# Expert gates of 13 batches computed as sums on VectorE, with list building moved and two layouts changed

## The reference

```python
x = x + tanh(g_xattn) * attention(ctx_1024, layernorm(x))   # 8 heads of 128; keys: context and latents, 512 in all
n = layernorm(x)
gates = (n @ Wg + bg) / (1 + 1e-6)                          # 256 features -> 8 experts
weights, indices = top_k(gates, 2); weights = softmax(weights)
h = silu(n @ W1[e] + b1[e]);  y = h @ W2[e] + b2[e]         # per expert e, 256 -> 1024 -> 256
x = x + tanh(g_ffn) * sum(weights * y[indices])
```

## Time and profile before

| what | value |
|---|---|
| median of 3 runs | 1513.13 us (1512.32 to 1515.56) |
| profiled execution, its own time | 1508.33 us |
| its span, first to last instruction | 1506.6 us |
| PE busy | 1483.4 us (98%) |
| DVE busy | 1165.3 us (77%) |
| ACT busy | 950.7 us (63%) |
| POOL busy | 581.0 us (39%) |
| granted TensorE clock, mean | 0.998 |

### The profile page before, as it was taken

The page is one execution under the profiler, slowest core; times in us unless marked ns, Lnnn a source line. Parts: engine busy times, 40 slices in busy tenths (PEclk is TensorE's granted clock), DMA queues, the critical chain, the costliest instruction groups (busy, mean ns, idle before and its releaser), DMA issues. The chain is left out here.

```text
span 1506.6 us, 29833 instructions
## 1 busy us (share of the span) xinstructions
PE 1483.4 (98%) x10326; PEld 1369.4 (91%) x10326; DVE 1165.3 (77%) x2753; ACT 950.7 (63%) x2058; POOL 581.0 (39%) x650
## 2 busy tenths in 40 slices
PE   9999999999999999999999999999999999999997
PEld 7888898898898998888888989888999999999996
DVE  7888787878878787887878788777767776666685
ACT  6565556556565565655555565656778777777775
POOL 4323433233342323333333343223455455544552
PEclk9999999999999999999999999999999999999999
DMA  6010202011010110101011010002657655555563
GB/s 198 29 36 22 38 20 50 22 36 43 22 50 8 50 43 23 36 22 50 8 50 43 22 36 22 8 23 91 156 133 202 175 128 131 133 148 140 127 184 78
DMA packets 70576, 106.92 MB, mean 71 GB/s; under 512 B 11513, under 2 KB 55606, under 8 KB 70302
## 3 DMA queue, kind: packets, MB, share of 16 engines
q1 hardware_dynamic: 54462, 85.98, 17.4%
q0 software_dynamic: 15824, 18.98, 8.0%
q10 hardware_dynamic: 144, 0.05, 0.0%
HBM read 86.64 MB, written 18.35 MB: 70 GB/s over the span
## 5 line engine op out<-in xcount | busy, mean ns | idle before, releaser
L942 POOL TENSOR_SCALAR probs<-probs,rsum 128x512 f32<-128x512 f32 x256 | 176.0, 700 | 622.4 <-DVE rsum L1641 622.0
L1162 ACT ACTIVATE pt_hi<-turn 128x512 fp32r<-128x512 f32 x256 | 139.1, 595 | 238.5 <-PE turn L1318 232.7
L968 POOL DMA_INDIRECT out_rows<-yo,token x71 | 127.1, 1790 | 182.5 <-DVE yo L1817 163.7
L1766 DVE TENSOR_TENSOR ht_lo<-hs,ht_hi 128x512 fp32r<-128x512 f32 x142 | 98.2, 691 | 112.2 <-ACT ht_hi L1129 111.1
L1635 DVE TENSOR_REDUCE smax<-score 128x1 f32<-128x512 f32 x256 | 168.3, 684 | 8.5 <-PE score L195 8.3
L1061 ACT ACTIVATE probs<-score,nbias 128x512 f32<-128x512 f32 x256 | 173.2, 686 | 1.7 <-DVE nbias L1637 1.7
L1893 DVE TENSOR_TENSOR pt_lo<-turn,pt_hi 128x512 fp32r<-128x512 f32 x256 | 164.3, 683 | 12.2 <-ACT pt_hi L1162 12.2
L1120 ACT ACTIVATE hs<-ph,vecs 128x256 f32<-128x256 f32 (+1 forms) x284 | 114.4, 458 | 88.7 <-PE ph L195 81.9
L193 PE MATMUL py<-w_hi,ht_lo 128*128 (+1 forms) x568 | 162.6, 286 | 2.2 <-DVE ht_lo L1766 2.2
L194 PE MATMUL py<-w_lo,ht_hi 128*128 (+1 forms) x568 | 160.6, 283 | 0.0
L195 PE MATMUL py<-w_hi,ht_hi 128*128 (+1 forms) x568 | 160.6, 283 | 0.0
(11 more groups left out here) (246 smaller groups left out, 4720.7 us busy)
## 6 DMA issues: line engine op xcount, KB each, us to landing
w_raw<-in_L_ffn_W SPq DMA_DIRECT2D x45, 1024.0 KB, 5.2
spread<-mean_and_factor SPq DMA_DIRECT2D x15, 512.0 KB, 3.6
xhat_rows<-rows SPq DMA_DIRECT2D x16, 264.0 KB, 2.2
x_raw<-in_x SPq DMA_DIRECT2D x16, 256.0 KB, 3.0
c_raw<-in_ctx SPq DMA_DIRECT2D x16, 256.0 KB, 3.2
out_rows<-x SPq DMA_DIRECT2D x16, 256.0 KB, 2.2
z_turned<-in_x_turned SPq DMA_DIRECT2D x15, 256.0 KB, 3.9
z_turned<-in_ctx_turned SPq DMA_DIRECT2D x15, 256.0 KB, 4.4
```

What stands on the lines that cost most here:

```text
L942: last = pool.tensor_scalar(probs[n % 2][:, t, :], probs[n % 2][:, t, :], rsum[:, n % 2, t:t + 1], 1.0, ALU.mult, ALU.mult)
L968: pool.indirect_dma_start(out=A["out"], out_offset=bass.IndirectOffsetOnAxis(ap=token[:, u:u + 1].bitcast(U32), axis=0), in_=yo_of(t)[:, s ...
L1162: act.activation(pt[0][:, 2 * t:2 * t + 2, :], turn[t][:, :].rearrange("p (j i) -> p j i", j=2), ACT.Copy).then_inc(s_pthi, 1)
L1766: dve.tensor_tensor(lo[:, :], hs[n % N_HS][:, :], hi[:, :].bitcast(F32), ALU.subtract).then_inc(s_hlo, 1)
```

## The change

1. For batches 0 to 12 the units "t" and "g" are gone from PE, and so is ACT's copy of "t". `dots` computes each gate on DVE: one `scalar_tensor_tensor` multiplies 256 features of a row by the weights of one expert and sums them into `gates`. 16 such instructions make a batch (8 experts, 2 tiles of rows): in step 3, three behind `kt_lo` and one ahead of `ot_lo`; in each of steps 4 and 5, one ahead of `kt_lo`, three behind it, one ahead of `ot_lo` and one behind it. `largest` adds the bias itself.
2. For these batches `largest`, `choose` and `weigh`, ACT's `exp_gap` and the unit "r" come one step later, `find_places` in step 0 of the next batch, and `list_tokens` after step 5 of the next batch.
3. The counts use fp32r operands (`chosen`, and rounded copies of two constant matrices, made once by ACT).
4. From the second transfer on, means and factors are laid in DRAM by kind and row, so that `centre` and `normalise_turned` read contiguous values. They were 32 bytes apart. The write is now two transfers of single values.
5. The gate weights are loaded once, spread over all partitions (1 MB), early in the kernel.

```diff
+DOT_B = EARLY_B - 1
...
-        if h == T_STEP and 1 <= b < B:
+        if h == T_STEP and DOT_B < b < B:
             units.append(("t", b - 1))
-        if h == G_STEP and 1 <= b < B:
+        if h == G_STEP and DOT_B < b < B:
             units.append(("g", b - 1))
-        if h == W_STEP and 1 <= b < B:
+        if h == (W_STEP if b > DOT_B else W_STEP + 1) and 1 <= b < B:
             units.append(("r", b - 1))
...
-            spread=nc.dram_tensor("mean_and_factor", (B, P, 2, JT), F32, kind="Internal").ap(),
+            spread=nc.dram_tensor("mean_and_factor", (B, 2 * KEYS), F32, kind="Internal").ap(),
...
-        chosen = late("chosen", [P, E, TT])
+        chosen = late("chosen", [P, E, TT], F32R)
...
+        below_r = late("below_r", [P, P], F32R)
+        ones_r = late("ones_r", [P, P], F32R)
...
+        wg_wide = sb("wg_wide", [P, E, D])
+        dot_junk = sb("dot_junk", [P, 4, D])
...
+                if c == 1:
+                    sp.dma_start(dram["spread"][c].rearrange("(i n) -> i n", n=2 * JT),
+                                 norms[:, :, :].rearrange("i r j -> i (r j)")).then_inc(s_norms_out, 16)
+                else:
+                    by_kind = dram["spread"][c].rearrange("(r j i) -> r i j", r=2, j=JT)
+                    with nc.allow_non_contiguous_dma(reason="a value of each row"):
+                        for r in range(2):
+                            sp.dma_start(by_kind[r], norms[:, r, :]).then_inc(s_norms_out, 16)
+                sp.wait_ge(s_norms_out, norms_out(c))
                 if c == 1:
                     weights_split(sp, "k1")
                 else:
                     sp.wait_ge(s_zin, KD * (c - 1))
-                sp.dma_start(spread[:, :, :, :].rearrange("p i r j -> p (i r j)"),
-                             dram["spread"][c].rearrange("i r j -> (i r j)").partition_broadcast(P)).then_inc(s_spread, 16)
...
+            weights_split(sp, "o1")
+            sp.dma_start(wg_wide[:, :, :].rearrange("p e d -> p (e d)"),
+                         A["gate_rows"].rearrange("e d -> (e d)").partition_broadcast(P)).then_inc(s_wg_wide, 16)
...
-                if h == L_STEP and 1 <= b < B:
+                if h == L_STEP and DOT_B < b < B:
                     list_tokens(b - 1)
+                if h == G_STEP + 1 and 2 <= b < DOT_B + 1 or i == H * (DOT_B + 1):
+                    list_tokens(b - 2)
...
+                    act.wait_ge(s_routing, N_ROUTING)
+                    act.activation(below_r[:, :], below[:, :], ACT.Copy).then_inc(s_round, 1)
+                    act.activation(ones_r[:, :], ones[:, :], ACT.Copy).then_inc(s_round, 1)
...
-                if i % H == E_STEP and 1 <= i // H < B:
+                if i % H == (E_STEP if i // H > DOT_B else E_STEP + 1) and 1 <= i // H < B:
                     exp_gap(i // H - 1)
...
-                    pe.wait_ge(s_routing, N_ROUTING)
+                    pe.wait_ge(s_round, 2)
                     pe.wait_ge(s_chosen, at + 1)
                     ch = chosen[:, :, :].rearrange("p e t -> p (e t)")
-                    pe.matmul(dst[:, 0:E * TT], below[:, :], ch, start=True, stop=True)
-                    last = pe.matmul(dst[:, E * TT:2 * E * TT], ones[:, :], ch, start=True, stop=True)
+                    pe.matmul(dst[:, 0:E * TT], below_r[:, :], ch, start=True, stop=True)
+                    last = pe.matmul(dst[:, E * TT:2 * E * TT], ones_r[:, :], ch, start=True, stop=True)
...
+            def dots(b, first, end):
+                dve.wait_ge(s_xn, b + 1)
+                dve.wait_ge(s_wg_wide, 16)
+                own.wait()
+                for q in range(first, end):
+                    e, t = divmod(q, TT)
+                    own.mark(dve.scalar_tensor_tensor(out=dot_junk[:, q % 4, :], in0=rows[b % 2][:, t, 0:D], scalar=1.0,
+                                                      in1=wg_wide[:, e, :], op0=ALU.mult, op1=ALU.mult,
+                                                      accum_out=gates[:, t, e:e + 1]))
             def largest(b):
-                dve.wait_ge(s_read, read_number["g", b] + 1)
+                if b < DOT_B:
+                    own.wait()
+                    own.mark(dve.tensor_tensor(gates[:, :, :], gates[:, :, :],
+                                               bg[:, :].unsqueeze(1).to_broadcast([P, TT, E]), ALU.add))
+                    own.wait()
+                else:
+                    dve.wait_ge(s_read, read_number["g", b] + 1)
...
-                own.mark(dve.tensor_tensor(by_rows, by_rows, spread[:, :, 0, :].rearrange("p i j -> p j i"), ALU.add))
+                own.mark(dve.tensor_tensor(by_rows, by_rows, spread_of(c, 0), ALU.add))
             def normalise_turned(c, k):
                 own.wait()
                 by_rows = zin[:, k, :].rearrange("p (j i) -> p j i", j=JT)
-                dve.tensor_tensor(by_rows, by_rows, spread[:, :, 1, :].rearrange("p i j -> p j i"), ALU.mult).then_inc(s_zin, 1)
+                dve.tensor_tensor(by_rows, by_rows, spread_of(c, 1), ALU.mult).then_inc(s_zin, 1)
             for i in range(STEPS + 2):
                 b, h = i // H, i % H
...
                 if i == STEPS:
                     lo_h(0)
                     find_places(B - 2)
+                summed = 1 <= b <= DOT_B
+                if summed and h == G_STEP:
+                    dots(b - 1, 4, 5)
+                if summed and h == G_STEP + 1:
+                    dots(b - 1, 10, 11)
                 for u in steps[i]:
                     if u[0] in "kq":
                         read_unit(*u)
...
                             normalise_turned(b + 1, 1)
                         if h == R_STEP + 1 and 1 <= b < B:
                             x2_moments(b - 1)
+                        if summed and h == T_STEP:
+                            dots(b - 1, 0, 3)
+                        if summed and h == G_STEP:
+                            dots(b - 1, 5, 8)
+                        if summed and h == G_STEP + 1:
+                            dots(b - 1, 11, 14)
                 if i < STEPS:
                     reciprocal_sum(i)
                 if i == STEPS - 1:
...
                 if i in (2, 3):
                     normalise_turned(1, i - 2)
                 for u in steps[i]:
+                    if u[0] == "o" and summed and h == T_STEP:
+                        dots(b - 1, 3, 4)
+                    if u[0] == "o" and summed and h == G_STEP:
+                        dots(b - 1, 8, 9)
+                    if u[0] == "o" and summed and h == G_STEP + 1:
+                        dots(b - 1, 14, 15)
                     if u[0] in "vogr":
                         read_unit(*u)
+                if summed and h == G_STEP:
+                    dots(b - 1, 9, 10)
+                if summed and h == G_STEP + 1:
+                    dots(b - 1, 15, 16)
                 if i == 0:
                     lo_weights(dve, "dve", "q1")
...
                 if 1 <= b < B:
                     for at, part in ((R_STEP, residual), (G_STEP, largest), (E_STEP, choose), (W_STEP, weigh),
                                      (L_STEP, find_places)):
-                        if h == at and i != STEPS - 1:
+                        if h == at + (summed and at >= G_STEP) and i != STEPS - 1:
                             part(b - 1)
+                if h == 0 and 2 <= b < DOT_B + 2:
+                    find_places(b - 2)
                 if i == HOME_STEP:
                     find_home()
                 if i == GATHER_STEP - 1:
...
+    arrays["in_gate_rows"] = np.ascontiguousarray(np.asarray(inputs["L0_ffn_Wg"]).T)
```

More of the change, by code:

```diff
@@ L442, in layer @@
                        o0=alloc(raws, "o0_raw", [P, H // 2, D]), o1=alloc(raws, "o1_raw", [P, H // 2, D]))
-        spread = sb("spread", [P, P, 2, JT])
+        spread = sb("spread", [P, 2 * KEYS])
+        wg_wide = sb("wg_wide", [P, E, D])
+        dot_junk = sb("dot_junk", [P, 4, D])
         x2, rows = [x2_0, x2_1], [rows0, rows1]
@@ L529, in layer @@
         s_padz, s_chosen, s_place, s_routing = sem("padding_zero"), sem("chosen"), sem("places"), sem("routing_consts")
+        s_round = sem("routing_consts_rounded")
+        s_wg_wide = sem("gate_weights_wide_in")
         s_dve, s_pool = sem("dve_self"), sem("pool_self")
@@ L644, in added, with norms_out, spread_of @@
             return min(t, WIDE) if half else t
+        def norms_out(c):
+            return 16 + 32 * (c - 1)
+        def spread_of(c, r):
+            if c == 1:
+                return spread[:, :].rearrange("p (i r j) -> p r j i", r=2, j=JT)[:, r]
+            return spread[:, :].rearrange("p (r j i) -> p r j i", r=2, j=JT)[:, r]
         def by_step(function, t):
@@ L739, in spread_norms @@
                 sp.wait_ge(s_z, c + 1)
-                sp.dma_start(dram["spread"][c], norms[:, :, :]).then_inc(s_norms_out, 16)
-                sp.wait_ge(s_norms_out, 16 * c)
+                if c == 1:
```

(9 more changed lines are left out.)

## The result

| | median | range | runs |
|---|---|---|---|
| before | 1513.37 us | 1512.32 to 1515.56 | 5 |
| after | 1505.12 us | 1500.99 to 1506.03 | 5 |

The ratio is 0.9935, 95% interval [0.9925, 0.9945]: faster by 0.65%, some 8 us. I had forecast 1517 and gave "faster" 0.38. The profiled execution took 1503.53 us, its span is 1501.8; against the profiled one of before that is -4.8.

The account below looks back on a forecast made before the run. PE was taken to bound the kernel: 20.8 us gained there against 13 batches of 1.9 us waiting gave +3.9 on 1508.3, 1512.2. With the median 4.8 above the profiled execution, the forecast was 1517, range 1490 to 1534.

Parts of the forecast that it names:

- What leaves PE: On PE, "t" and "g" save 1.31 us per batch, "r" 0.25; together 20.8 us, between 17.0 and 24.4.
- In place: one engine waits for the other: Steps 3 to 5: DVE's dots and POOL's work exclude each other on shared ports, making PE wait 1.9 us per batch.
- POOL's pair isn't opened: Rival: both halves of POOL's normalisation run before a waiting dot; 3.5 us per batch, 1538; chance 0.16.
- So a dot costs 0.45 to 0.56 and I take 0.45 to 0.50: DVE's time for each dot including the accumulator's read, 7.2 to 8.0 us per batch.
- The walk: One batch followed through steps 3 to 6 on DVE and POOL: 1.7 us of waits at 0.45 a dot, 2.4 at 0.50.
- the transposes' share: In step 5 PE's transposes wait for POOL's pair, delayed by dots: another 0.4 us per batch.
- The sum: PE's gain of 20.8 us against 13 batches of 1.9 us waiting: +3.9 us on the profiled execution.
- my likeliest case: Waits between 1.7 and 2.4 us per batch in steps 3 to 6: 1510 to 1527, chance 0.42.
- the hidden dots: Rival: POOL doesn't hold the dots, 1492; hidden in whole or good part, 1490 to 1508, chance 0.34.
- the point from which it decides: Waits below 1.6 us per batch, 20.8/13, decide for the rival that the dots are hidden.
- What is moved, all at nothing: List transfers, later routing work, new layout of means and factors, gate weights and ACT's copies: no cost.

Follow-up runs that it names:

- x1: Changed kernel with POOL's subtraction `kvt_lo` left out from batch 2 on, so later batches use an old low part; 1498.99 us, ratio 0.9889.
- x2: Changed kernel with the same 16 dots per batch moved within steps 3 to 5, none around `kt_lo` in step 4; 1502.9 us, ratio 0.991.
- x3: Kernel before with only the counts changed to fp32r operands; 1514.24 us, ratio 0.9989.
- x5: Changed kernel with the dots' scalar read from a column of ones in SBUF instead of the constant 1.0; 1511.34 us, ratio 0.9979.
- x4: Changed kernel with means and factors laid as before, 32 bytes apart and written in one transfer; 1509.66 us, ratio 0.9958.
- x12: x2 with the four list transfers in two pairs, behind POOL's pairs of the third and sixth steps; 1485.22 us, ratio 0.9824.
- x13: x2 with one list transfer each behind POOL's pairs of the third, fifth, sixth and seventh steps; 1484.83 us, ratio 0.9823.
- x14b: Changed kernel, dots where the change put them, with the list transfers in two pairs as in x12; 1502.34 us, ratio 0.9907.
- x8: x2 with the four list transfers one step earlier, behind POOL's pair of the fifth step; 1564.42 us, ratio 1.0317.
- x6: Changed kernel with each batch's four list transfers issued in the step after the first of a batch; 1554.62 us, ratio 1.026.
- x11: x2 with the four list transfers behind POOL's pair of the eighth step; 1587.94 us, ratio 1.0478.

## Why the prediction was wrong, point by point

- **What leaves PE** was right. "t" and "g" leave steps 3 to 5 at 7.9 where nothing disturbs them (x1, x2): the full 1.31. "r" gave 0.22 (x3), where I had taken 0.25.
- **In place: one engine waits for the other** was right in mechanism, in the instructions it named and in their order. Step 4's dots wait behind `kvt_hi` and `kvt_lo`, the next scores for `qt_lo`, the pair of POOL is opened by a dot (so the rival *POOL's pair isn't opened* is out), and the transposes of step 5 start 1.70 into it instead of 1.39. The Trainium skill (SBUF — State Buffer, section "SBUF: two separate sides") has VectorE with two SBUF inputs and GpSimd exclude each other for a whole instruction; this trace agrees for the dots, 1.95 beside `kvt_lo` and 0.41 without it (x1).
- **The step that failed: "So a dot costs 0.45 to 0.56 and I take 0.45 to 0.50".** It is 0.345, 16 dots 5.5 us and not 7.2 to 8.0. 0.06 of the difference is the scalar from SBUF (x5), the rest the accumulator read, which I had added and which costs no time. The walk built on this price fails with it: "The three dots behind `kt_lo` then run from 7.3 to 8.65", 1.35 us behind POOL's end. They took 0.90, as the dot that had waited held the next instruction only 0.21 behind POOL's end and the other two 0.345 each. With cheap dots the chain ahead of POOL's split is not late: `mv_a` is at 1.17 of step 4 where I had 1.6, `kt_lo` at 4.61 and not 5.1 (o isn't late at all), `kvt_lo` ends at 6.95 and not 7.4. Scores wait 0.48 instead of 1.3, the transposes' share is 0.39 with what follows instead of 0.4, and step 6 gets nothing. Together 0.87 per batch for 1.9. The price alone isn't the whole miss. By the 0.22 per batch that 0.06 per dot brought in x5, dots at 0.45 to 0.50 would give some 1.25 to 1.45 per batch (my estimate, a straight line from x5), where the walk had 1.7 to 2.4. The rest is the walk itself, which made the held dot and the delay ahead of POOL's split too long; no run takes these apart.
- **The sum** with that term: -20.8 + 13 by 0.87 (11.3) = -9.5, 1503.6 from the median of 1513.1. Measured were 1505.1 and, on the second chip, 0.9949. That it comes out so near is in part luck: the sum knows neither the 4.5 us that the profile loses in the second stage nor the long step, whose place and length changed. The result is between my likeliest case and the hidden dots, within the 1490 to 1508 to which I gave 0.34: the waits are below the 1.6 us per batch that I had named as the point from which it decides, and so the change gained where I had forecast a loss.
- **What is moved, all at nothing.** Right for the layouts (x4), wrong for the list transfers. Nothing waits for them in the steady state at the place they have, but every profile with four in a row in the sixth step has a stall behind the first group, of 3.8 to 7.7 us for ACT (4.4 in the kernel before), and at three of the five places tried the same transfers cost 47 to 87 us more. I had looked at POOL's time for them (5.4 us) and not at how long the transfers themselves stay in the way. The Trainium skill (DMA: Bandwidth & Descriptors, section "Specifications") says that pieces under 512 bytes are written by read-modify-write; the lists are pieces of 4 bytes, and no run here changes their size. The Trainium skill gives a first-byte latency of about 1 us for transfers from GpSimd in the same section. In the changed kernel the first packet of the lists is recorded 1.8 us and the first semaphore update 2.3 us after POOL began the first issue, and the 22 to 26 us of a first group of four lie mostly behind that.

## What stays open

Why ACT and PE themselves stand in the long step isn't shown: no transfer of data that they wait for is in the trace at that time. That it is tied to the lists rests on the time (ACT stands at some time between 10 and 23 us after the first of a group in every first-stage stall), on its absence in x12, x13 and x14b, and on the updates of the list transfers. In the changed kernel 34 of the first group's 64 are recorded, none between 207.5 and 215.6, and ACT stands from 210.15 to 214.53. In the kernel before none is recorded between 162.8 and 170.2 (ACT: 164.96 to 169.32), in x2 none between 208.1 and 216.1 (ACT: 208.24 to 215.94). Whether the updates stop there or only their records are lost, the traces don't say; x12, without a stall, has all 1024.

From the first score pass of the last step to the end, three profiles (before, x12, x13) take 447 to 449 us, the others 451 to 455, x3 among them, which shares only the counts with the change. It costs the changed kernel 4.5 us in its profile. The time is in stalls of ACT of the same kind, 4.7 us together, which those three profiles don't have:

```profile
1086.66 0.84 ACT L1154 ACTIVATE hs<-ph,vecs 128x256 f32<-128x256 f32 x2 [1.59 <-remote]
...
1108.70 0.84 ACT L1154 ACTIVATE hs<-ph,vecs 128x256 f32<-128x256 f32 x2 [3.09 <-remote]
```

No run here was aimed at them. x14b keeps the second (3.19), though its lists of the first stage go in pairs, and x12, with the same pairs, has neither.

## What to carry to other kernels

Price an instruction by a row with the same kinds of operands, and look for the start of the next one, not for the sum of its records: here 0.345 against 0.45 to 0.50 was the largest single error behind a forecast of the wrong sign. The indirect transfers of small pieces here were complete long after POOL had issued them; count what starts behind such a transfer, and try spreading them rather than issuing four in a row. And when dots or other two-input work fill DVE's gaps, put them into steps where POOL is idle.

## What was not expected of the hardware

- A `scalar_tensor_tensor` with accumulation over 256 values and a constant scalar is followed by the next after 0.345 us, with a scalar from SBUF after 0.405.
- Four indirect writes of 4-byte pieces, issued within 5 us, are complete up to 25.9 us after the first (x8), two up to 12.0 (x12), and the first single one after 6.5 (x13). The first of four loads of 256 KB, issued 8.3 us after the first of four writes, was used after 16.1 us instead of 6.0 (x6). In pairs nothing waits for them; one by one, `z_turned` waits for its factors twice, 0.5 and 0.7 us.
- The same group gets quicker in the course of an execution, from 22.1 to 12.4 us in x11; the pairs of x12 from 12.0 to 6.5. The cause isn't known.
- After PE had stood 4.2 us (x2) its granted clock was 0.50 in the next 4 us; after 0.66 us (the changed kernel) it stayed at 1.00.
